# Eight in place of four buffers of gathered rows in a graph kernel's edge sums

## The reference, cut to what matters

```python
for i in range(weight.shape[0]):          # three rounds
    m = h @ weight[i]
    agg = segment_sum(m[src], dst, n_nodes)
    h = gru_cell(agg, h, w_ih, w_hh, b_ih, b_hh)
...
agg_sum = segment_sum(x[src], dst, n)     # last layer
agg_mean = agg_sum / maximum(counts, 1.0)[:, None]
h = concatenate([x, agg_mean], axis=-1) @ weight
```

## Time and profile before

| | |
|---|---|
| time, median of 3 runs | 6054.59 us (6049.87 to 6078.45) |
| time of the profiled execution | 6070.21 us |
| span of its core in the trace | 6068.3 us |
| PE matmul / DVE / ACT / POOL busy | 72% / 68% / 46% / 60% |
| mean granted TensorE clock | 0.865 |
| DMA moved over the span | 802.51 MB, mean 132 GB/s |
| first to last gather start, gate0, gate1 | 3363.8 to 3672.9, 4002.3 to 4299.8 us |
| first to last gather start, gate2, mean3 | 4609.1 to 4975.2, 5352.9 to 5689.7 us |

### The profile page before, as it was taken

The page is one execution under the profiler, slowest core; times in us unless marked ns, Lnnn a source line. Parts: engine busy times, 40 slices in busy tenths (PEclk is TensorE's granted clock), DMA queues, the critical chain, the costliest instruction groups (busy, mean ns, idle before and its releaser), DMA issues. The chain is left out here.

```text
span 6068.3 us, 76920 instructions
## 1 busy us (share of the span) xinstructions
PE 4367.1 (72%) x16790; PEld 2619.4 (43%) x16790; DVE 4101.2 (68%) x13622; ACT 2768.2 (46%) x6238; POOL 3623.7 (60%) x3234
## 2 busy tenths in 40 slices
PE   6688859999998565545666579977896669936643
PEld 3355544444444333334444344534443334436643
DVE  6566658999998544447776576557665889836633
ACT  0233326777776010136666345534443446536643
POOL 4665638888886788845555661046204757855455
PEclk8787769999999777778888899989998889968876
DMA  6222223333332343356665575457544667757621
GB/s 213 62 76 72 73 66 88 99 100 98 98 98 75 74 62 62 59 102 198 187 199 181 169 210 161 131 150 216 172 141 141 176 161 204 202 163 226 190 78 54
DMA packets 767746, 802.51 MB, mean 132 GB/s; under 512 B 139776, under 2 KB 527944, under 8 KB 767162
## 3 DMA queue, kind: packets, MB, share of 16 engines
q1 hardware_dynamic: 405498, 393.44, 22.9%
q0 software_dynamic: 117504, 209.42, 14.6%
q10 hardware_dynamic: 244288, 194.72, 9.6%
HBM read 445.32 MB, written 351.92 MB: 131 GB/s over the span
## 5 line engine op out<-in xcount | busy, mean ns | idle before, releaser
L462 PE MATMUL gate_bank<-gate_ht,gate_whh 128*128 128x512 f32 x1764 | 872.4, 618 | 28.6 <-DVE gate_n L532 15.8
L925 POOL DMA_INDIRECT xh<-mean_xh,mean_pos_all x392 | 378.4, 965 | 338.9 <-DVE mean_xh L1027 142.2
L462 PEld LDWEIGHTS gate_bank<-gate_ht,gate_whh 128*128 128x128 f32 x1764 | 341.8, 202 | 407.0 <-issue 384.7
L2080 PE MATMUL back_ps_sums<-back_same,back_rows 128*128 128x512 f32 x400 | 286.6, 883 | 291.5 <-DMA back_rows<-x_a,back_idx 291.5
L151 POOL DMA_INDIRECT ffn_rows<-att_sums,ffn_idx x392 | 409.6, 1045 | 114.8 <-issue 106.3
L289 POOL DMA_INDIRECT gate_rows<-h_a,by_pos x200 | 197.8, 989 | 429.0 <-POOLq L117 328.4
L1521 PE MATMUL ffn_ps_f<-ffn_hg,ffn_f 128*128 128x512 f32 x784 | 407.1, 616 | 47.6 <-ACT ffn_hg L1698 47.6
L458 PE MATMUL gate_bank<-by_rank,gate_win 128*128 128x512 f32 x882 | 436.0, 594 | 0.0
L1514 PE MATMUL ffn_ps_u<-ffn_xs_t,ffn_up_w 128*128 128x512 f32 x784 | 387.0, 596 | 1.1 <-issue 1.1
L2061 POOL DMA_INDIRECT back<-back_out,back_dest x200 | 324.1, 1620 | 67.8 <-issue 60.1
L583 ACT ACTIVATE gate_z<-gate_bank,gate_b_rz 128x512 f32<-128x512 f32 x294 | 201.5, 685 | 346.0 <-PE gate_bank L462 225.6
(11 more groups left out here) (273 smaller groups left out, 12080.1 us busy)
## 6 DMA issues: line engine op xcount, KB each, us to landing
mean_x<-x_a SPq DMA_DIRECT2D x196, 256.0 KB
back<-blank ACTq DMA_DIRECT2D x99, 264.0 KB, 4.5
mean_rows<-back SPq DMA_DIRECT2D x98, 264.0 KB
hp<-mean_xh SPq DMA_DIRECT2D x98, 264.0 KB
gate_x<-xh SPq DMA_DIRECT2D x98, 264.0 KB
gate_hot<-hot_rows SPq DMA_DIRECT2D x100, 256.0 KB
ffn_x<-in_x_in SPq DMA_DIRECT2D x98, 256.0 KB
ffn_xr<-in_x_in SPq DMA_DIRECT2D x98, 256.0 KB
```

What stands on the lines that cost most here:

```text
L462: last = nc.tensor.matmul(bank_[:, :], whh[:, c * D:(c + 1) * D], ht[:, t.slot4, :], start=not inputs, stop=True)
L925: nc.gpsimd.indirect_dma_start(out=g["xh"][:, :], out_offset=bass.IndirectOffsetOnAxis(ap=pos_all[:, t.n, j:j + 1], axis=0), in_=xh[:, t.n ...
L2080: last = nc.tensor.matmul(ps_sums[t.slot][:, :], rows[:, t.slot4, j, :], same[:, t.slot, j, :], start=j == 0, stop=j == J - 1)
```

## The change

The buffers for gathered rows, and the semaphores that say a buffer is full, become eight in place of four; POOL waits for the sum (and the copied positions) of tile n-8 in place of n-4. Nothing else is altered: the same instructions in the same order on every engine.

```diff
@@ class SegmentSums @@
-        self.rows = f.sb("rows", [P, 4, J, width])
+        self.rows = f.sb("rows", [P, 8, J, width])
...
-        self.gathered = f.sems("gathered", 4)
+        self.gathered = f.sems("gathered", 8)
...
     def gather(self, pool, t):
-        wait(pool, self.summed, t.n - 3)
+        wait(pool, self.summed, t.n - 7)
         if self.carries:
-            wait(pool, self.placed, t.n - 3)
+            wait(pool, self.placed, t.n - 7)
...
-                out=self.rows[:, t.slot4, j, :], out_offset=None, in_=self.table[:, :],
+                out=self.rows[:, t.n % 8, j, :], out_offset=None, in_=self.table[:, :],
...
-            ).then_inc(self.gathered[t.slot4], 16)
+            ).then_inc(self.gathered[t.n % 8], 16)
...
-        wait(pe, self.gathered[t.slot4], 64 * (t.u4 + 1))
+        wait(pe, self.gathered[t.n % 8], 64 * (t.n // 8 + 1))
...
-                                         self.rows[:, t.slot4, j, 0:D],
+                                         self.rows[:, t.n % 8, j, 0:D],
...
-            wait(dve, self.gathered[t.slot4], 64 * (t.u4 + 1))
-            self.nc.vector.tensor_copy(self.g["by_pos"][:, t.n, :], self.rows[:, t.slot4, :, D]
+            wait(dve, self.gathered[t.n % 8], 64 * (t.n // 8 + 1))
+            self.nc.vector.tensor_copy(self.g["by_pos"][:, t.n, :], self.rows[:, t.n % 8, :, D]
```

## The result

| | before | after |
|---|---|---|
| time, median | 6064.54 us (6049.87 to 6078.45, 4 runs) | 6131.21 us (6118.77 to 6138.37, 4 runs) |
| profiled execution | 6070.21 us | 6138.37 us |
| mean granted TensorE clock | 0.865 | 0.858 |

The kernel got slower: the ratio is 1.0107, with a 95% interval of 1.0089 to 1.0125. The forecast was 6055 us with a range up to 6088. It was read against the median of three runs of before, 6054.59 us; with the fourth run, 6074.49, that median is 6064.54. What came is rival (A), held at 8%: it gave +65 us, and the medians differ by 66.7.

A forecast was written before the change was run, and what follows sets the result against it. First halves bound by gate0's compute loop and gate1's busy DVE, not by gathers, whose rows have 14 us to land. All terms 0: profiled 6070.21 us less 0, read against the 6054.59 median, gives 6055 us, range 6035 to 6088.

The forecast's parts named there:

- rival (A): Stage starts: the pause lasts as long as POOL streams gathers, 20 us more in three stages, 5 in gate2; 6120 us; 8%.
- (1): All stages: no instructions added but four semaphores to clear per stage, behind the barrier; counted as nothing.
- (2): gate0, gate1, mean3: POOL's waits for buffers go, on nobody's path; lead gained over 29, 22, 11 steps; worth 0.
- (3): gate2: the norm at line 224 holds POOL three steps ahead whatever the number of buffers; worth 0.
- (4): Transfers while POOL catches up: same bytes, four tiles per stage earlier; from 15 us lost to 7 us gained, taken as 0.
- (B): While POOL catches up: slower by DMA contention alone, not given back; +15 us, 6070 us; 12%.
- (C): PE's sums: the 83.4 us of "issue" idle is hidden waiting for rows and mostly goes; about 5980 us; 3%.
- (D): PE's pauses and ends of the halves: transfers spread, ends free of gathers; 7 us or a little more gained, 6045; 12%.
- (E): POOL's lead: another wait holds it at four tiles, so the change does nothing; the time is the forecast again.
- A2: Later theory from the experiments: each tile of lead costs about 5 us whenever gained, PE's results being seen late during unbroken gathers.

The follow-up runs named there:

- The early half alone: Eight buffers, eight tiles ahead up to tile 11 of each stage, then four, against the kernel before: 0.9993 and 1.0001, both on prompt occasions.

## Why the prediction was wrong

**Instructions** (1): right; the buffers and semaphores alone cost nothing (1.0001).

**POOL's waits, worth 0** (2): this step failed. Two assumptions carried it. The first was that POOL catches up slowly, 29, 22 and 11 steps long, while the others go on. In the run POOL gained all four tiles in the pause at the start, when nobody used rows, and stood at its new limit with tile 10 (11 in gate1); its waits were back at once (33.4 + 13.9 us in gate1), and in gate1 its last gather came 297.8 us after the first, as before (297.5), not 24 us earlier. The second was that POOL's work costs only POOL. The rows were there: 24 gathers, then ACT; 3.58 us of ACT and 2.37 us of POOL ending together. I named these pauses waits for PE and didn't ask what PE's lateness goes with. (Two slips in the sums change nothing in the forecast: gate1's 22 steps take 5.07 us of POOL's work per tile where the text has 5.0, which gives 20, and the lower bound of the traffic uses gate1's step for mean3 too.)

**gate2** (3): right beyond the first tiles: the norm of line 224 holds POOL back (eight from tile 16 on 745.3, four ahead 744.6 us). At the start POOL may issue one tile more, 28 gathers for 24, and gate2 became 5.2 us longer.

**Traffic** (4): the bounds of +15 and -7 us were about the wrong resource. The DMA share of the windows didn't rise (0.71, 0.70, 0.62 and 0.69 against those of the earlier trace rows) and was 0.21 in the pause. The rule of the Trainium skill, "DMA: Bandwidth & Descriptors", section "Issuing engines are not separate DMA queues", that transfers started by the scalar, sync and gpsimd engines interleave on the same 16 DMA engines, isn't contradicted by this, but it isn't what cost the time.

**Rival (A)**, 8%: its mechanism and its size were right, 20, 20, 5 and 20 us against 22.6, 22.3, 5.2 and 19.2, on an occasion on which PE's results come late. The argument against it (DVE goes on in the middle of the stream of mean3) weighed too much: PE's results are late, not stopped, so one getting through excludes nothing. Its wording, that the results are seen only when POOL has stopped, is too strong for the same reason: at 4067.45 and 4072.99 POOL was still streaming. And it is narrower than what was found, since the lead costs the same when it is gained later. **(B), (C), (D)** have no sign in the traces: PE's idle time put down to "issue" before line 321 grew, from 83.4 to 108.9 us, with the pauses.

**(E)** didn't apply: POOL did get eight tiles ahead in three stages.

Open: why PE's results come late on some occasions only; the runs don't show what differs. That three tiles ahead save 5 us per stage on a late occasion follows from A2, but none was met with it, so no version is shown to be better than the kernel before. The early half alone was not seen on a late occasion either, and that leaves a reading untested which the expectation for it names: that POOL's own 200 gathers set the pace there, and only the tiles left after the last gather count. On the late occasions the rest of gate0 after its last gather is 353 to 354 us long in the kernels that end with eight ahead (353.7 in the changed one) and 329 in those that end with four (329.4 before), while the last gather doesn't come sooner. Both readings fit the measured ratios; they part on whether a lead that is given back has cost anything. Nor do the runs separate POOL's issuing of a gather from the transfer of its rows, which always go together.

## What to carry to other kernels

A producer that runs further ahead than its consumer needs isn't free: building the lead takes its own time once, and where the producer's issuing holds up somebody else, that time is on the path, whether it is spent at a stage's start or later. So first read how early the data lie ready (14 us here), and give no buffers if nobody waits for them. If everybody pauses for an engine that has finished its work, look for what runs without a break in that pause, and measure the change on more than one occasion.

## What the runs showed of the hardware

While POOL issued indirect DMAs without a break (one per 1.25 us), PE's results were seen late by ACT, DVE, POOL and SP on the late occasions: ACT's first sigmoid started 25.3 us after its product, and POOL went on 39.2 us after the end of the sum that it waited for (4047.14 to 4086.36), with five signals coming in order, 5.5 to 7 us apart. With 20.64 us of additions on POOL in place of gathers the steps went on. What DVE, ACT or a DMA signals to PE wasn't late: PE went on 0.05 us after the end of DVE's operation (4072.99 + 0.75 and 4073.79), and its first sums started with the landing of their rows. On the prompt occasions the first sigmoid started 2.0 us after its product under the same stream, and the whole kernel, unchanged in its instructions, took 5562 to 5566 us in place of 6064 to 6097. PE was busy 4394.7 us in the changed kernel's profile on a late occasion and 4236.1 on a prompt one, DVE 4098.2 and 4092.7; so most of the 573 us between the two executions is waiting.
